# ScalarE's attention loop of 30 passes over two units written out as 64 units in a row

## The reference

```python
# layer 0: B=2, C=256, H=W=64, 8 heads of 32 channels, num = 4096 positions
q = proj(Wq, bq) / math.sqrt(hd)
k = proj(Wk, bk)
v = proj(Wv, bv)
attn = jax.nn.softmax(jnp.einsum('bnd,bmd->bnm', q, k), axis=-1)
fuse = jnp.einsum('bnm,bmd->bnd', attn, v)
hybrid = _conv1x1(jnp.concatenate([x, fuse], axis=1), Wf, bf)
x = hybrid * m + x * (1.0 - m)
# layer 1 follows: depthwise 3x3, relu, gate, 1x1, depthwise 3x3, 1x1, times x
```

## Time and profile before

| | us |
|---|---|
| median of three runs | 4376.66 |
| lowest and highest | 4370.67, 4379.80 |
| the profiled execution | 4380.74 |
| its span, first to last instruction | 4378.9 |
| its units 2 to 60 on ScalarE | 3339.35 |

### The profile page before, as it was taken

The page is one execution under the profiler, slowest core; times in us unless marked ns, Lnnn a source line. Parts: engine busy times, 40 slices in busy tenths (PEclk is TensorE's granted clock), DMA queues, the critical chain, the costliest instruction groups (busy, mean ns, idle before and its releaser), DMA issues. The chain is left out here.

```text
span 4378.9 us, 80623 instructions
## 1 busy us (share of the span) xinstructions
PE 3920.1 (90%) x19317; PEld 2054.6 (47%) x19317; DVE 3055.1 (70%) x5030; ACT 2937.0 (67%) x5512; POOL 2964.1 (68%) x1360
## 2 busy tenths in 40 slices
PE   7869999999989999999899989999999999969887
PEld 4535444444444444444454445544444444524333
DVE  3257777777767777777677767777777777727989
ACT  1228777777777777777677777777777777850313
POOL 3427778778878778887687788777777777870000
PEclk9959999999999999999899999999999999989999
DMA  6932211221112112211121112211221111112021
GB/s 208 286 69 38 39 20 21 40 38 18 19 28 40 30 20 30 40 30 21 31 40 30 21 18 37 37 20 20 40 39 20 21 21 20 16 48 82 19 77 39
DMA packets 298174, 189.55 MB, mean 43 GB/s; under 512 B 199186, under 2 KB 223940, under 8 KB 297668
## 3 DMA queue, kind: packets, MB, share of 16 engines
q1 hardware_dynamic: 297860, 186.20, 21.5%
HBM read 124.32 MB, written 61.47 MB: 42 GB/s over the span
## 5 line engine op out<-in xcount | busy, mean ns | idle before, releaser
L875 DVE TENSOR_REDUCE block_max<-mx 128x1 f32<-128x512 f32 (+1 forms) x3584 | 2527.0, 761 | 1000.4 <-PE mx L676 982.2
L816 ACT ACTIVATE prob<-st 128x512 f32<-128x512 f32 x4096 | 2134.0, 606 | 736.4 <-PE st L665 506.1
L665 PE MATMUL st<-queries,keys 97*128 97x512 f32 x4096 | 1637.1, 421 | 238.6 <-ACT prob L816 203.4
L515 POOL TENSOR_TENSOR prob_sum<-prob_sum,prob 128x1024 f32<-128x1024 f32 x768 | 1823.5, 2390 | 20.3 <-POOL prob_sum L515 18.6
L676 PE MATMUL mx<-keys,max_queries 96*128 96x512 f32 x4096 | 1611.1, 420 | 86.3 <-ACT tail_exp L806 51.1
L515 POOL TENSOR_TENSOR prob_sum<-prob 128x1024 f32<-128x1024 f32 x384 | 915.3, 2384 | 765.1 <-PE acc L708 690.2
L665 PEld LDWEIGHTS st<-queries,keys 97*128 97x128 f32 x4096 | 789.5, 194 | 822.4 <-ACT prob L816 381.7
L676 PEld LDWEIGHTS mx<-keys,max_queries 96*128 96x128 f32 x4096 | 810.5, 198 | 464.2 <-ACT tail_exp L806 205.9
L688 PE MATMUL acc<-prob,values 128*32 128x512 f32 x8192 | 1025.4, 620 | 0.0
L806 ACT ACTIVATE tail_exp<-mx,negated_max 128x1024 f32<-128x1024 f32 x512 | 574.0, 1121 | 106.7 <-DVE negated_max L879 87.5
L688 PEld LDWEIGHTS acc<-prob,values 128*32 128x32 f32 x8192 | 219.3, 112 | 503.1 <-ACT prob L816 254.7
(11 more groups left out here) (106 smaller groups left out, 1279.8 us busy)
## 6 DMA issues: line engine op xcount, KB each, us to landing
max_queries<-q_scratch SPq DMA_DIRECT2D x384, 64.0 KB
queries<-q_scratch SPq DMA_DIRECT2D x384, 64.0 KB
keys<-k_scratch SPq DMA_DIRECT2D x168, 128.0 KB, 5.2
x<-in_x SPq DMA_DIRECT2D x18, 512.0 KB, 3.7
q_scratch<-high SPq DMA_DIRECT2D x32, 256.0 KB, 4.5
k_scratch<-high SPq DMA_DIRECT2D x16, 512.0 KB, 4.9
q_scratch<-low SPq DMA_DIRECT2D x32, 256.0 KB, 4.9
k_scratch<-low SPq DMA_DIRECT2D x16, 512.0 KB, 4.7
```

The source lines that it names most:

```text
L515: nc.gpsimd.tensor_tensor(psum[k][:, :, :], a, prob[:, (first + i) % RING, :, :], ALU.add).then_inc(added[False], 1)
L665: nc.tensor.matmul(st[bank(i, p)][:, :], kk[gp][:, h, s * P:(s + 1) * P], qq[p][:, h, :], start=True, stop=True).then_inc(scores, 1)
L816: nc.scalar.activation(prob[:, s % RING, h, :], st[bank(i, p)][:, :], ACT.Exp).then_inc(exp_done, 1)
L875: nc.vector.tensor_reduce(bmax[p][:, hn, k:k + 1], banks.rearrange("p b n -> p (b n)"), AX.X, ALU.max, negate=True).then_inc(mx_taken, 1)
```

## The change

ScalarE's loop is gone. All 64 units are written out by a Python loop when the program is built, with the same arguments as before: no `prev` in unit 0, two units ahead up to unit 61, one in unit 62, none in unit 63. Every wait is now for a constant. ScalarE's attention program is 7,492 instructions (before: 133 ahead of the loop, 404 in it, and what follows it): the 4,801 of the engine as before, 2,689 waits as instructions of their own, one table load ahead and one branch behind. No register operation is left in it. No other engine's program changes.

```diff
--- before.py
+++ after.py
@@ -829,13 +829,8 @@
             nc.scalar.activation(warm[:, :], ones[:, 0:1], ACT.Exp)
             for n in range(HN + TAIL_FIRST):
                 sum_tail(n // HN, n // HN, n % HN, first=n < HN)
-            unit(0, 0, prev=False)
-            with act.Fori(0, UNITS // 2 - 2) as u2:
-                unit(u2 * 2 + 1, 1)
-                unit(u2 * 2 + 2, 0)
-            unit(UNITS - 3, 1)
-            unit(UNITS - 2, 0, ahead=1)
-            unit(UNITS - 1, 1, ahead=0)
+            for u in range(UNITS):
+                unit(u, u % 2, prev=u > 0, ahead=min(2, UNITS - 1 - u))
             copy_num(UNITS - 1)
             copy_den(UNITS - 1)
```

## The result

The changed kernel takes 4081.07 us (median of four runs, 4071.72 to 4084.22), the kernel before beside it 4375.24 us. The ratio is 0.9324, with a 95% interval of 0.9305 to 0.9343: faster by 294 us. The forecast was 4178 us, a gain of 199, with a range of 4095 to 4245.

The account below looks back on a forecast made before the run. TensorE was taken to bound the units, with ScalarE's loop pause lengthening every second one. 59 x 52.80 plus 15.3 plus 9.65 gave 3140 us instead of 3339, so 4376.7 - 199 = 4178 us, range 4095 to 4245.

Parts of the forecast that it names:

- What bounds the kernel: Attention units 2 to 60: TensorE sets 51.65 us each; ScalarE's pause behind its loop branch makes every second unit 8.2 us longer.
- The stretch: Units 2 to 60 in ScalarE's loop: predicted to fall from 3339 to 3140 us, a gain of 199 us.
- 59 x the full-clock unit: Units 2 to 60: a unit at full TensorE clock takes 51.65 us, read from sixteen even units.
- A third of the units with a slow spell: Units 2 to 60: one in three meets TensorE's low clock and takes 55.10 us, making the average unit 52.80 us.
- Units 16, 32 and the DMA wait: TensorE's outer branches at units 16 and 32 keep 15.3 us excess; the late maxima row before unit 40 keeps 9.65 us.
- The register operations: ScalarE's 211 register instructions per pass go: between 7 us more and 31 us less, taken as nothing.
- The longer program: ScalarE's 7,492 straight instructions are fetched once: nothing gained or lost in bandwidth, and no late fetches expected.
- the slower rival: ScalarE's straight code pauses as well; with one pause in each unit 4594 us, chance 0.06.
- Covers that go: With the pause gone GpSimd has 5.7 us to spare in a unit and VectorE 10.7; neither becomes the bound.
- All units clean: Rival: low clock in even units goes with the loop's pause, all 59 take 51.65 us; 4109 us, chance 0.20.
- the last two: Rivals: ScalarE's straight code pauses too, 4594 us, chance 0.06; the pause is not the loop's, 4377 us, chance 0.04.

Follow-up runs that it names:

- shift16: The kernel before, loop kept, with 16 always-satisfied idle instructions put ahead of ScalarE's attention loop: 4120.52 us, ratio 0.9413.

## Why the prediction came out 97 us too high

**What bounds the kernel: right in the main.** The pause belonged to the loop, it cost the odd units some 8 us each, and the slow clock followed from TensorE's idle time. The runs with idle instructions and with fewer branches show the first, the pause put back shows the other two. Of the 294 us the pauses and their clock are 238 by the run that puts them back and 257 by the run that takes them out and keeps the branch; the runs' spread is about as large as the difference.

**The stretch.** The forecast for units 2 to 60 was 3140 us and the trace has 3035.4. (The spans of the profiled executions are 302 apart where the medians are 294; hence 105 here and 97 above.) The 105 us fall to three terms of the sum.

*59 x the full-clock unit: mis-sized, 65 us.* I took 51.65 us from sixteen even units as TensorE's pace because TensorE was busy for 50.97 of it. Measured: 50.54 over the 46 full-clock units of the changed kernel, so 1.11 x 59 = 65 us. The even units were no clean sample, and this reading of them is the step that failed. The branch stands at their end, and the join with the next odd unit cost them about a microsecond, which the trace put down to TensorE: 2.02 us in the earlier trace rows and 1.04 after. With the pause shifted away but the branch kept, full-clock even units take 1042.55 / 20 = 52.13 us and odd ones 1261.22 / 25 = 50.45; with neither branch nor pause they are equal. A pair is 102.58 us there, 101.76 with 30-unit passes and 101.08 in straight code: 0.82 us of join and 0.68 of register operations, 24 and 20 us over the stretch. The other 21 us are that the longer kind of unit stood for both kinds: the even and odd units of that run are 51.29 us at the mean, 0.36 less than 51.65. That "TensorE is busy", 98.7% of these units, was true and proved nothing, for these stretches hold more than a unit's work of TensorE. By when they start, 286 matmuls fall into such an even unit of the kernel before, 274 into an odd one, and 280 into an even or odd unit of the changed kernel; the counts in the rows say it too, x288 to x292 in the even units of the earlier trace rows, and x281 in the earlier trace rows and in the stretches after. At full clock a matmul has 0.178 us of busy time in both kernels, so six more are 1.1 us, as much as the error.

*A third of the units with a slow spell: mis-sized, 37 us.* I carried one in three over from the even units. After, ten of the 56 units other than 16, 32 and 39 have one, 53.69 us each where a clean one takes 50.54: 31 us instead of 68. It was right that such spells don't need ScalarE's pause, and wrong to take their rate for a constant. They become fewer as TensorE's and then the others' loops go: ten, then five, two and none, in one trace each; VectorE's and GpSimd's loops alone leave nine, and the version without any loop has one.

*Units 16, 32 and the DMA wait: right in size, 3 us, wrong in cause.* 15.3 + 9.65 = 25 us kept, 22 us measured. The 9.65 us were a DMA that came late, but no accident that "may not come again": it comes at this unit in every trace with TensorE's loops, and in none without.

**The register operations: taken at nothing, were 20 us.** The bounds of +7 and -31 us hold the value. Units 61 and 62 were a poor measure: they are straight code, but they were set beside 51.65, which was itself too high, and the changed kernel's own 61 and 62 take 51.1 and 50.7 us.

**The longer program: right.** No wait without a cause longer than 0.5 us stands in 7,492 instructions in a row (one of 3.1 us in unit 47 is put down to "remote", as two are in shift16), and the slower rival has nothing for it. By the rule of the Trainium skill that I set beside it ("Runtime: NRT & Kernel Launch", section "Instruction fetch mechanics") prefetch in sequence is hidden, and the straight runs agree. The same rule has the stall come before execution can go on at the target. Here only the longer join of about 1 us and a few waits of 2.6 to 6.2 us stand there; the pause comes 13 instructions later, on the piece of code that follows, and 16 idle instructions ahead of the loop do away with it.

**Covers that go: right.** GpSimd is busy 44.8 us of 51.45, VectorE 40.6, and TensorE's scores wait for the exponentials 33.3 us in all. Neither has become the bound.

**The rivals.** "All units clean", 4109 us, was nearest, at a chance of 0.20, and even its range stopped at 4095. The recorded sum is also wrong there: 4109 less the 31 us of its own bound on the register work is 4078, which would have taken in the measured time, though by luck: that rival gives all units a full clock, and ten had a slow spell. All my cases but the last two stood on this one number or on units read like it, and so the range was too narrow where it mattered: a bound on the clean unit was missing. Such a bound was in reach: the trace of before has 2.75 us at the joins with the branch against 1.78 at those without it, and 30 x 0.97 = 29 us would have moved the low end to 4066.

## What to carry to other kernels

A loop's branch costs at more places than the gap that the trace calls by no name. Here it paused the engine some instructions into the body, stretched the step at the join that is booked under another engine, and brought TensorE's clock down behind it. So when units of a loop serve as the sample for straight code, take none that ends or begins at a branch, or bound the difference, and count the busiest engine's instructions in the sample: more of them than the unit's share mean that it borrowed work from its neighbour. And before unrolling at the price of a long program, move the loop by some idle instructions: here 16 of them gave 257 of 294 us, and 112 gave 124, so the place has to be searched. Where one engine's loop paid, try the loops of the other engines too: they brought another 114 us here.

## What I had not expected of the hardware

- The cost of a branch back depends on where the loop lies: 6.7 us a pass as it was, nothing but the longer join with 16 instructions more ahead, and 3.6 to 4.7 us with 112 more.
- One of the 128 completions of a row of maxima came 9.5 us behind the others, at the same unit in all eight traces with TensorE's loops, and in none once they were written out, with the DMAs as before.
- A gap of 7.1 us between two score exponentials, filled with real instructions, is followed by TensorE at half clock for some 10 us, as the loop's pause is; the unit is 8.4 us longer, 1.3 more than the gap.
- Loops of VectorE and GpSimd brought 6 us alone, within the noise, and 23 us once TensorE's were straight. Whether they gain more together is not shown.

Open: what sets off the ten slow spells of the changed kernel; why the piece behind the target takes 6.7 us to come, when its packet starts, at the median, only 2.6 us before ScalarE goes on (in units 31, 35, 37 and 47 the packet itself takes 5.3 to 7.8 us where the median of such packets is 0.44, and SyncE's loads of queries run at this time; whether they hold it up, no run tests); and by which way TensorE's loops cost the 62 us, of which 24 are the three units, some 20 the shorter clean unit and 16 the slow spells.
